# Order of loads, split of the input and opening of a three-direction recurrence on one core

## What is computed

```python
def _gru_step(x, h, wih, whh):
    gi, gh = x @ wih.T, h @ whh.T
    ir, iz, i_n = jnp.split(gi, 3, axis=-1)
    hr, hz, h_n = jnp.split(gh, 3, axis=-1)
    r, z = jax.nn.sigmoid(ir + hr), jax.nn.sigmoid(iz + hz)
    n = jnp.tanh(i_n + r * h_n)
    return (1.0 - z) * n + z * h
def step(h, xr):
    ctx = _gru_step(xr, h, wih, whh)          # kept: the context of this line
    return jnp.tanh(_conv1d(ctx, cw, cb)), ctx # three taps along the line
...
out = x + einsum(concat(ctx_above, ctx_below, ctx_left), w_comb) + b_comb
```

## Time and profile before

| | us |
|---|---|
| three runs, median (lowest to highest) | 380.04 (379.86 to 380.16) |
| the profiled execution | 380.04 |
| its span (first to last instruction) | 377.6 |
| PE busy in the span | 339.0 (90%) |
| DVE busy | 294.2 (78%) |
| ACT busy | 258.2 (68%) |
| GpSimd busy | 14.3 (4%) |

### The profile page before, as it was taken

One profiled execution on the slowest core, in us unless ns is written; L12 is line 12 of the kernel. 1 busy time (PEld: TensorE's weight loads), 2 busy tenths in 40 slices (PEclk: granted clock), 3 DMA queues, 4 the chain that ended last, 5 costly groups with the idle time before them and its releaser, 6 DMA issues.

```text
span 377.6 us, 7679 instructions
## 1 busy us (share of the span) xinstructions
PE 339.0 (90%) x2718; PEld 265.1 (70%) x2718; DVE 294.2 (78%) x776; ACT 258.2 (68%) x584; POOL 14.3 (4%) x28
## 2 busy tenths in 40 slices
PE   0356869997999999999999999999999999999995
PEld 0113647776777777777888888888888888884442
DVE  1817577987888888889888888888888888887432
ACT  4557566777777777777777777777777777775700
POOL 2560000000000000000000000000000000000000
PEclk9996878999999999999999999999999999999999
DMA  7800000000000000000000000000000000000554
GB/s 305 348 0 1 3 0 2 0 2 0 3 1 2 2 1 2 2 1 2 2 1 2 0 0 0 0 0 0 0 0 0 0 0 0 0 0 2 167 143 136
DMA packets 10212, 10.63 MB, mean 28 GB/s; under 512 B 464, under 2 KB 8784, under 8 KB 10192
## 3 DMA queue, kind: packets, MB, share of 16 engines
q1 hardware_dynamic: 10192, 10.36, 8.0%
HBM read 6.16 MB, written 4.19 MB: 27 GB/s over the span
## 4 chain that ended last, share of the span: by engine, by line
PE 69%; DVE 16%; ACT 7%; issue 2%; POOL 2%; DMA 2%; POOLq 0%; SPq 0%; ACTq 0%
PE rz_bank L806 19%; PE conv_bank L806 13%; PE rz_bank L809 9%; PE n_bank L806 8%; PE conv_bank L809 7%; ACT rz L481 4%; PE n_bank L809 4%; DVE npre L692 2%; DVE context L685 2%; DVE npre L704 2%; DVE ctx_store L697 2%; DVE x_rows L610 2%; DVE nval L677 2%; DVE rz L715 2%; DVE h_parts L709 2%
## 5 line engine op out<-in xcount | busy, mean ns | idle before, releaser
L806 PE MATMUL conv_bank<-ctx_store,w_parts 128*128 (+1 forms) x558 | 108.8, 276 | 2.2 <-issue 2.2
L806 PE MATMUL rz_bank<-x_rows,w_parts 128*128 128x256 f16 (+1 forms) x384 | 84.7, 283 | 12.0 <-DVE x_rows L610 11.6
L806 PE MATMUL rz_bank<-h_parts,w_parts 128*128 128x256 f16 x372 | 77.5, 276 | 0.0
L481 ACT ACTIVATE rz<-rz_bank,descale 128x512 f32<-128x512 f32 x96 | 66.0, 687 | 16.0 <-PE rz_bank L806 8.0
L493 ACT ACTIVATE nval<-npre 128x256 f32<-128x256 f32 x93 | 38.7, 416 | 54.7 <-DVE npre L704 54.7
L692 DVE SCALAR_TENSOR_TENSOR npre<-n_bank,descale,rz 128x256 f32<-128x256 f32 x93 | 45.0, 484 | 33.9 <-ACT rz L481 33.9
L809 PE MATMUL conv_bank<-ctx_store,w_parts 128*128 (+1 forms) x279 | 67.4, 277 | 0.0
L806 PEld LDWEIGHTS conv_bank<-ctx_store,w_parts 128*128 128x128 f16 x558 | 55.2, 99 | 11.2 <-issue 2.5
L498 ACT ACTIVATE hval<-conv_bank,biases,descale 128x256 f32<-128x256 f32 x93 | 52.3, 562 | 11.9 <-PE conv_bank L806 11.1
L806 PEld LDWEIGHTS rz_bank<-x_rows,w_parts 128*128 128x128 f16 x384 | 37.7, 98 | 28.1 <-DVE x_rows L610 21.1
L809 PE MATMUL rz_bank<-x_rows,w_parts 128*128 128x256 f16 (+1 forms) x192 | 54.3, 283 | 0.0
(11 more groups left out here) (91 smaller groups left out, 413.1 us busy)
## 6 DMA issues: line engine op xcount, KB each, us to landing
x<-x_dram SPq DMA_DIRECT2D x8, 512.0 KB, 8.4
out_dram<-x_rows SPq DMA_DIRECT2D x8, 512.0 KB, 3.2
ctx_store<-weights_dram SPq DMA_DIRECT2D x3, 576.0 KB, 5.0
ctx_store<-weights_dram SPq DMA_DIRECT2D x1, 192.0 KB, 12.1
biases<-biases_dram SPq DMA_DIRECT2D x1, 2.0 KB, 11.7
```

The source lines that it names most:

```text
L481: nc.scalar.activation(rz[k][:].rearrange("p g c -> p (g c)"), rz_bank[k][:], ACT.Sigmoid, scale=gate_scale(k)).then_inc(sig_done[k], 1)
L806: last = nc.tensor.matmul(out, w_block(HI, k, n), parts(hi_or_lo), start=start, stop=stop and hi_or_lo == LO, skip_group_check=True)
```

## The change

1. **Loads.** The weights of direction 1 are loaded behind the images. The first group of weight sets is that of direction 0 alone (`SET_GROUPS = ((0, 2), (2, SETS))`), and ACT takes the magnitudes of direction 1 behind image 4.
2. **GpSimd apart.** GpSimd makes only the low parts of direction 0's three units, from a scaled copy of its own; ACT rounds all units straight from the loaded weights with the scale in the instruction, and no longer waits for GpSimd. The units of direction 1 go to DVE.
3. **Layout.** `x_norm` holds two images interleaved (writes go to every second element); `x_rows` is row, column, image, so that a row is 256 elements in a row. The loop can then take one step per iteration, 16 iterations.
4. **Pieces.** A ring is two single columns and four rows, in blocks up to four earlier than their use, and PE waits for just the pieces that a line needs (`pieces_until`). The first input products of a direction run the passes with the high part before they wait for the low part.
5. **Opening.** The first blocks, up to (1, 0) on ACT and DVE and (1, 1) on PE, are written out in an order of their own on each engine. The unit "comb" is moved from block (4, 0) to (14, 1). `LAST_WARM` is 7 for 4.

```diff
-SET_GROUPS = ((0, 4), (4, SETS))
+SET_GROUPS = ((0, 2), (2, SETS))
-FRONT_WARM, CHAIN_WARM, LAST_WARM = 12, 4, 4
+FRONT_WARM, CHAIN_WARM, LAST_WARM = 12, 4, 7
...
+    columns = [Cells((lo, end), (col, col + 1)) for col in (width - 1, width - 2)]
+    rows = [Cells((row, row + 1), (0, width - 2)) for row in (lo, end - 1, lo + 1, end - 2)]
+    return columns + rows
...
-        x_rows = sb("x_rows", [C, 2, H, W // 2, B, 2], f16)
+        x_rows = sb("x_rows", [C, 2, H, W, B], f16)
...
-        x_norm = stored[:, half:half + 2 * B * SPACE].bitcast(f32).rearrange("p (b h w) -> p b h w", b=B, h=H)
+        x_norm = stored[:, half:half + 2 * B * SPACE].bitcast(f32) \
+            .rearrange("p (e h w o) -> p e h w o", e=B // 2, h=H, o=2)
...
+            with eng.Fori(UNROLLED, STEPS - 1) as t:
                 for j in range(DIRS):
                     block(t, j)
...
             load_weights(0)
-            load_weights(1)
             for b in range(B):
                 sp.dma_start(x32[:, b, :, :], x_d[b, :, :, :]).then_inc(x_loaded[b], 16)
-            for k in (2, COMB):
+            for k in (1, 2, COMB):
                 load_weights(k)
...
-                nc.gpsimd.tensor_tensor(out=merged(w32[:, lo:hi, :]), in0=merged(w32[:, lo:hi, :]),
+                nc.gpsimd.tensor_tensor(out=w_scaled32[:, unit, :], in0=merged(w32[:, lo:hi, :]),
                                         in1=w_scale[:, n:n + 1].to_broadcast([C, GATES * C]), op=ALU.mult) \
...
-                if unit < len(POOL_UNITS):
-                    act.wait_ge(w_scaled, unit + 1)
...
+                act.wait_ge(scale_done, 1 if n < SET_GROUPS[0][1] else 2)
+                nc.scalar.activation(w_parts[:, HI, lo:hi, :], w32[:, lo:hi, :], ACT.Copy,
+                                     scale=w_scale[:, n:n + 1]).then_inc(w_hi_done, 1)
...
-                nc.scalar.activation(cells(x_norm[:, b, :, :]), cells(x32[:, b, :, :]), ACT.Identity,
+                nc.scalar.activation(cells(x_norm[:, b // 2, :, :, b % 2]), cells(x32[:, b, :, :]), ACT.Identity,
...
             warm(CHAIN_WARM)
+            warm(CHAIN_WARM)
+            pe.wait_ge(x_factor, 1)
             turn_sums(1)
-            pe.wait_ge(x_factor, 1)
             warm(LAST_WARM)
             spread_peaks(1)
...
+                if isinstance(s, int) and s < UNROLLED:
+                    if k == 2:
+                        column = line(k, s)
+                        needed = pieces_until(slice(0, H), slice(column, column + 1))
+                    else:
+                        needed = pieces_until(slice(line(k, s), line(k, s) + 1), slice(0, W))
+                    if first:
+                        unit_ready(f"in {k}")
+                        pe.wait_ge(x_hi_done, needed)
+                    else:
+                        pe.wait_ge(x_lo_done, needed)
```

280 lines of the change are left out of this document (158 added, 122 removed).

## The result

| | before, us | changed, us |
|---|---|---|
| median of the runs (lowest to highest) | 380.10 (379.86 to 380.37) | 353.16 (352.12 to 354.0) |
| the profiled execution | 380.04 | 352.87 |
| its span | 377.6 | 351.2 |
| `x_shift` written (end of the head) | 29.00 | 20.68 |
| from there to the sigmoid of direction 2's step 2 | 39.35 | 38.03 |

The ratio of changed to before is 0.929 (95% interval 0.9263 to 0.9317). The forecast was 356.7 us with a range of 353.0 to 362.8; the median lies inside it, 0.16 us above its lower end.

What follows compares the result with a forecast made beforehand. Bounds: GpSimd's power in the head, no full engine in the opening, waits for DVE's pieces in the unrolled steps, PE in the loop. Span 377.6 - 7.3 + 0.3 - 13.1 + 0.3 - 3.6 = 354.2, plus 2.44: 356.7 us, range 353.0 to 362.8.

Steps and rivals of the forecast that it cites:

- Head: Start of the kernel until x_shift is written: ends at 21.7 us for 29.0, 7.3 us less.
- rival 3: Head gains only half, since ACT's magnitudes or the loads come last: 360.3 us, chance 0.06.
- Opening: From x_shift to the sigmoid of direction 2's step 2: 39.7 us for 39.35, 0.3 us more.
- two waits: PE in the opening: 41.0 to 43.5 us for a bank behind ACT's cores, 46.2 to 50.0 for row 2's piece.
- Two stretches of 3.4 us at 1.2 GHz: Opening: PE's clock falls after idle times of 2.4 and 3.8 us, moving the closing sigmoid from 58.9 to 61.4.
- The interleaved write: Normalisation in the opening: write keeps its speed, taken at nothing; at the pieces' rate, opening 0.8 to 1.3 us longer.
- Unrolled steps: Eleven steps after the opening: PE's waits for pieces go, 97.4 us for 110.5, 13.1 us less.
- Rivals 2 and 5: 2: DVE's chain sets 3.15 us a block, 363.3 us, chance 0.12; 5: PE's piece count still tight, 367.5 us, 0.04.
- Loop: The 53 blocks after the unrolled steps: 2.95 us each, 156.4 us for 160.1, 3.6 us less; "comb" priced separately.
- rival 1: Layout brings PE nothing, row groups of input products stay at 1.08 us: 361.9 us, chance 0.11.
- rival 4: Loop ends no longer covered with one every step; slower than before from 1.5 us an end, chance 0.01.
- Outside the span: Execution time around the profiled span: taken as 2.44 us, as in the kernel before.

Runs made afterwards that it cites:

- e5_pool: The changed kernel with four more GpSimd products behind its three pairs, written to an unused tile: 353.98 us.
- e3_row2: The changed kernel with row 2's piece split in block (1, 1) instead of (1, 2): 348.67 us.
- e9_loop2: The changed kernel with its loop written as two steps per iteration again: 353.38 us.
- e1_layout: The kernel before with only x_rows laid out as row, column, image: 396.86 us.
- e2_waits: The kernel before, with PE waiting in the first 15 steps for just the pieces its line needs: 369.96 us.
- e7_power: The kernel before with GpSimd's power of the variance after the fourth of its six units: 382.01 us.
- e8_inorder: The kernel before with x_rows as row, column, image and the pieces copied in the order of the destination: 380.09 us.

## Why the prediction was right, point by point

**Head: −7.3 forecast, −8.3 measured.** Loads, statistics, ACT's place off the path and GpSimd's free start came as told: the last statistics end at 16.88 for 16.7. `x_shift` was written at 20.68, sooner than the 21 to 22.5 that the prediction named as a sign of being right. The miss is one term, "2.93 us of averages and small operations, the same afterwards". From the last moments to the variance it is now 1.87 (16.88 to 18.75). Of the 1.06 that fell away, 1.07 is the two steps that had waited for GpSimd (0.66 and 0.75 for 0.17 each); e5_pool put half of that back. The row to look at was there before the run: an 8-element instruction at 0.75 us next to one at 0.16. ACT's magnitudes (done at 19.95) lay hidden, as forecast, and rival 3 (half a head) fell.

**Opening: +0.3 forecast, −1.3 measured.** The laid out lists gave the right places and causes of two waits: one for the bank behind ACT's cores and a new one for row 2's piece. Where the clock stays up in front of it, the first is 2.34 us (e3_row2, e9_loop2) for the forecast 2.5; in the changed kernel it is 1.42, since PE came to it later. The second is 3.48 for 3.8. The account of the clock is right in part only, and by luck in number. "Two stretches of 3.4 us at 1.2 GHz" were to follow these two waits. One did, from 48.4 into the window from 51. Behind the bank's wait the clock did not fall, not even behind the 2.34 us of e3_row2, and the other stretch lies where none was forecast, from 34.7 to 37.6, behind waits of 1.48 and 0.70 us. The two cost 1.45 us (10.27 less 8.82) and 0.42 (16.89 less 16.47), 1.9 together for the forecast 2.5 (61.4 less 58.9): 0.6 of the miss of 1.6. The first sigmoid came 3.75 us behind `x_shift` (24.43) for the forecast 4.0, another 0.25; the remaining 0.75 is spread over the lists. So an idle time of 2 us, from which the prediction took its falls, does not decide: the clock stayed up behind 2.34 us and fell behind 1.48 and 0.70, and the same code has the earlier fall in one trace and not in another.

The interleaved write, taken at nothing, costs nothing on DVE (712 for 713 ns) and 76 ns a core on ACT (1154 for 1078). The Trainium skill's page "Vector Engine (DVE) Microarchitecture Reference", section "Performance modes — why throughput varies by op and dtype", names no step as a condition for one source at two results a cycle, and for this write, f32 at a step of 8 bytes, the trace agrees. It does not carry over to the pieces, which have two sources: there the write of single f16 elements 16 bytes apart trebled the time in e1_layout.

**Unrolled steps: −13.1 forecast, −13.0 measured.** The waits for pieces are gone (e2_waits alone gives 7.3 of the 13.0), the layout gives its 0.09 us per row group, and PE bounds at 2.95 us a block with DVE close behind. Rivals 2 and 5 fell: a block takes 2.95, not 3.15, and DVE's wait for the sigmoid between 60 and 170 us shrank from 12.3 to 0.6 us. What the prediction lacked is the reason why the layout could be had at all; it took the price of the pieces as given, and e1_layout shows how near a threefold price lay.

**Loop: −3.3 forecast with "comb", −3.8 measured.** "Comb" stands in block (14, 1), so in this stretch, at 165.45 on DVE; the prediction added 0.3 for it (its own 0.5 less 0.3 gives 0.2), and PE shows no wait there. Row groups at 0.98 (rival 1 fell, by e1_layout too) and no gap at the ends (rival 4 fell, by e9_loop2).

**Outside the span: 0 forecast, −0.8 measured.** The time of an execution less its span is 2.44 us in the kernel before and 2.2 to 2.5 in every execution of e1_layout, e2_waits, e7_power and e8_inorder; it is 1.67 in the changed kernel and 1.67 to 1.79 in every execution of the seven made from it. So it is not the layout alone, the waits alone, the power's place, the order of loads, row 2's piece, "comb" or the form of the loop. What it is stays open; no run tells it.

The sum of the misses is 1.0 + 1.6 − 0.1 + 0.5 + 0.8 = 3.8 us, which is 356.7 less 352.87. No miss over 0.1 us lay on the other side, so the time ended at the very edge of the range. The mechanisms of the head, the steps and the loop were right. The small steps of the head were mis-sized, the place of one fall of the clock was wrong, and the time outside the span was missing.
